# Graph layer with pre-norm on one core: layer-norm statistics, the last relu and add, and the last step of a count move from VectorE to ACT, POOL and PE

## The reference

```python
h = maximum(layernorm(x), 0)                 # eps 1e-5, over the 128 channels
mask = adj != 0
idx = the first 25 neighbours of each node, in order of their number
agg = h[idx].max(over the neighbours)        # with at most 25 neighbours also max(agg, 0)
out = x + relu(concat([h, agg], -1) @ W + b)
```

## Time and profile before

| | |
|---|---|
| median of 3 runs | 734.77 us (734.31 to 734.83) |
| profiled execution, its own time | 734.86 us |
| its span | 732.9 us |
| busy: DVE, PE, ACT, POOL | 91%, 85%, 65%, 7% of the span |
| mean granted TensorE clock | 0.971 |

### The profile page before, as it was taken

The page is one execution under the profiler, slowest core; times in us unless marked ns, Lnnn a source line. Parts: engine busy times, 40 slices in busy tenths (PEclk is TensorE's granted clock), DMA queues, the critical chain, the costliest instruction groups (busy, mean ns, idle before and its releaser), DMA issues.

```text
span 732.9 us, 10603 instructions
## 1 busy us (share of the span) xinstructions
PE 619.5 (85%) x3216; PEld 281.0 (38%) x3248; DVE 663.3 (91%) x941; ACT 476.1 (65%) x594; POOL 50.3 (7%) x41
## 2 busy tenths in 40 slices
PE   2278979899788997889899898989989898998976
PEld 2033443434334352443435343343525334353423
DVE  2559999999998999989998999989999999989996
ACT  2588568783777737775676857778478837858220
POOL 1300002000110002100030000200021000300000
PEclk9689999999999999999999999999999999999998
DMA  9240131410315103151302413141122410030100
GB/s 365 70 169 34 58 144 43 167 78 30 144 64 196 57 13 130 73 185 57 123 20 102 158 57 143 57 176 60 48 116 80 179 57 30 0 114 3 57 15 14
DMA packets 19125, 67.61 MB, mean 92 GB/s; under 512 B 4499, under 2 KB 7830, under 8 KB 16534
## 3 DMA queue, kind: packets, MB, share of 16 engines
q1 hardware_dynamic: 19094, 67.26, 24.4%
HBM read 42.08 MB, written 4.19 MB: 63 GB/s over the span
## 4 chain that ended last, share of the span: by engine, by line
DVE 40%; PE 35%; issue 17%; ACT 4%; DVEq 2%; DMA 1%; POOL 1%; ACTq 0%
DVE best L695 15%; PE picked L528 11%; PE picked L529 9%; DVE late_hot L701 7%; DVE prefix L232 5%; DVE hot L676 5%; PE ring L473 4%; PE side L487 4%; DVE best L796 4%; PE final L556 2%; PE final L560 2%; DVE late_most L681 1%; PE ring L479 1%; DVE late_other L684 1%; DMA adj_in<-in_adj_dram 1%
## 5 line engine op out<-in xcount | busy, mean ns | idle before, releaser
L695 DVE TENSOR_TENSOR best<-picked,best 128x1024 f32<-128x1024 f32 x224 | 268.8, 1217 | 22.4 <-PE picked L529 21.6
L528 PE MATMUL picked<-hot,h_hi 128*128 128x512 f16 x512 | 198.0, 387 | 57.7 <-DVE best L695 45.6
L529 PE MATMUL picked<-hot,h_lo 128*128 128x512 f16 x512 | 196.8, 384 | 0.0
L528 PE MATMUL picked<-late_hot,hi_skew 128*128 128x512 f16 x336 | 127.6, 380 | 13.0 <-DVE late_hot L701 8.6
L529 PE MATMUL picked<-late_hot,lo_skew 128*128 128x512 f16 x336 | 127.3, 379 | 0.0
L528 PEld LDWEIGHTS picked<-hot,h_hi 128*128 128x128 f16 x512 | 50.4, 98 | 160.0 <-DVE best L695 86.6
L796 DVE TENSOR_TENSOR best<-picked,best 128x1024 f32<-128x1024 f32 x84 | 102.4, 1219 | 8.4 <-PE picked L529 8.3
L361 ACT ACTIVATE rank<-ring,bias_big 128x512 bf16<-128x512 f32 x128 | 81.2, 683 | 28.5 <-PE ring L479 27.7
L400 ACT COPY best<-picked 128x1024 f32<-128x1024 f32 x32 | 32.3, 1015 | 101.9 <-PE picked L529 101.9
L676 DVE TENSOR_SCALAR hot<-rank 128x4096 f16<-128x4096 bf16 x64 | 90.1, 1409 | 7.7 <-ACT rank L361 7.7
L361 ACT ACTIVATE late_rank<-ring,late_bias 128x512 bf16<-128x512 f32 x128 | 81.0, 685 | 21.5 <-PE ring L479 15.2
(11 more groups left out here) (77 smaller groups left out, 560.6 us busy)
## 6 DMA issues: line engine op xcount, KB each, us to landing
adj_in<-in_adj_dram SPq DMA_DIRECT2D x16, 2048.0 KB, 7.9
late_skew<-late SPq DMA_DIRECT2D x32, 192.0 KB, 2.3
x_in<-in_x_dram SPq DMA_DIRECT2D x8, 512.0 KB, 8.6
xres<-in_x_dram SPq DMA_DIRECT2D x16, 256.0 KB, 7.8
late_skew<-late SPq DMA_DIRECT2D x16, 256.0 KB, 2.4
late_skew<-late SPq DMA_DIRECT2D x32, 128.0 KB, 2.0
out_dram<-xres SPq DMA_DIRECT2D x16, 256.0 KB, 2.0
late_skew<-late SPq DMA_DIRECT2D x32, 64.0 KB, 1.9
```

The lines of the kernel that those rows point to most:

```text
L528: nc.tensor.matmul(dst, hi[:, slot, k, :], onehot, start=start, stop=False)
L529: return nc.tensor.matmul(dst, lo[:, slot, k, :], onehot, start=False, stop=stop)
L695: nc.vector.tensor_tensor(best[:, half, s, :, :], picked[s][:, :, :], best[:, half, s, :, :], ALU.max).then_inc(picked_read, 1)
```

## The change

VectorE's `stats_of`, `moments_of` and `finish_group` go. ACT forms the statistics inside `spreads`: per class a Copy scaled by -1/C whose accumulator is minus the mean, then a Square with that as bias whose accumulator is the sum of squares, then the square root. It does so at the very front of its queue for batch 0, and for the next batch in the step of the even group, behind the last `make_mask` and in front of `first_maxima`. `make_gain` moves from use 8 to use 4, `relu_parts` from behind use 15 to use 8. The relu of the output is ACT's `cut_result`, last in its step, and the addition to x is POOL's `finish_group`. In the count, the four small operations into `late_other` go; PE's `tops`, behind pick 10, spreads the four partial maxima with two tiny matmuls into row 0 of `side`, and VectorE's `set_rounds` reduces these five numbers at use 11.

```diff
-    STATS_USES, MOMENTS_USE, SPREAD_USE, GAIN_USE = (4, 5), 6, 7, 8
+    GAIN_USE, RELU_USE = 4, 8
+    ROUNDS_USE = COUNT_USE + 2
...
             def normalize(batch):
                 pool.wait_ge(gain_made, 2 * batch + 2)
+                mean = minus_mean[:, :].unsqueeze(2).to_broadcast([P, K, C])
+                nc.gpsimd.tensor_tensor(h32[:, :, :], x_in[:, :, :], mean, ALU.add).then_inc(centred, 1)
...
+            def finish_group(g, s, loaded):
+                pool.wait_ge(xres_loaded[s], loaded)
+                pool.wait_ge(added_made, g + 1)
+                nc.gpsimd.tensor_tensor(xres[:, s, :], added[:, :], xres[:, s, :], ALU.add).then_inc(result_made, 1)
...
             def spreads(batch):
-                act.wait_ge(moments_made, K * batch + K)
-                nc.scalar.activation(spread[:, :], moments[:, :, 1], ACT.Sqrt, bias=bias_eps[:, 0:1]).then_inc(spread_made, 1)
+                act.wait_ge(x_loaded, 16 * batch + 16)
+                if not isinstance(batch, int) or batch > 0:
+                    act.wait_ge(lo_made, batch)
+                for k in range(K):
+                    nc.scalar.activation(h32[:, k, :], x_in[:, k, :], ACT.Copy, scale=-1.0 / C,
+                                         accum_out=minus_mean[:, k:k + 1]).then_inc(means_made, 1)
+                act.wait_ge(means_made, K * batch + K)
+                for k in range(K):
+                    nc.scalar.activation(h32[:, k, :], x_in[:, k, :], ACT.Square, bias=minus_mean[:, k:k + 1],
+                                         accum_out=squares[:, k:k + 1]).then_inc(squares_made, 1)
+                act.wait_ge(squares_made, K * batch + K)
+                nc.scalar.activation(spread[:, :], squares[:, :], ACT.Sqrt, bias=bias_eps[:, 0:1], scale=1.0 / C).then_inc(spread_made, 1)
...
+            def cut_result(g):
+                act.wait_ge(result_made, g + 1)
+                act.wait_ge(final_written, g + 1)
+                nc.scalar.activation(added[:, :], final[:, :], ACT.Relu).then_inc(added_made, 1)
...
+            spreads(0)
             for n in range(TURNS):
                 turned_mask(0, n)
...
-                    if use == SPREAD_USE and new_batch:
-                        spreads(batch)
-                if new_batch:
-                    relu_parts(batch, slot)
+                    if use == RELU_USE and new_batch:
+                        relu_parts(batch, slot)
...
+                if u % PER_BATCH == 0 and not at_end(it, u, PER_BATCH):
+                    spreads(batch_of(it, u) + 1)
                 if more:
                     for s in range(2):
                         first_maxima(g + 1, s, (u + 1) % 2)
...
+                cut_result(g)
...
+            def tops(g):
+                pe.wait_ge(late_reduced, g + 1)
+                nc.tensor.matmul(side[0:1, 0:CHAINS + 1], ones[:, 0:1], top_ones[:, :], start=True, stop=False)
+                nc.tensor.matmul(side[0:1, 0:CHAINS], late_most[:, :], eye32[:, 0:P:PART], start=False,
+                                 stop=True).then_inc(tops_written, 1)
...
                     pick_pair(g, use, slot)
                     if use == PAIRS and more:
                         lower_sums(at - TURNS)
+                    if use == COUNT_USE + 1:
+                        tops(g)
...
-            def count_rounds(g, s):
+            def count_rounds(g):
                 dve.wait_ge(count_written, g + 1)
                 nc.vector.tensor_reduce(late_most[:, :], side[:, :], AX.X, ALU.max).then_inc(late_reduced, 1)
-                dve.wait_ge(late_reduced, (CHAINS + 1) * g + 1)
-                for c in range(CHAINS):
-                    nc.vector.tensor_scalar(late_other[:, c:c + 1], late_most[c * PART:c * PART + 1, :], LINK * P / 2, 1.0, ALU.add,
-                                            ALU.max).then_inc(late_reduced, 1)
-                dve.wait_ge(late_reduced, (CHAINS + 1) * (g + 1))
-                nc.vector.tensor_reduce(late_rounds[0:1, s:s + 1], late_other[:, :], AX.X, ALU.max).then_inc(rounds_known, 1)
+
+            def set_rounds(g, s):
+                dve.wait_ge(tops_written, g + 1)
+                nc.vector.tensor_reduce(late_rounds[0:1, s:s + 1], side[0:1, 0:CHAINS + 1], AX.X, ALU.max).then_inc(rounds_known, 1)
...
-            def finish_group(g, s, loaded):
-                dve.wait_ge(final_written, g + 1)
-
-                dve.wait_ge(xres_loaded[s], loaded)
-                nc.vector.scalar_tensor_tensor(out=xres[:, s, :], in0=final[:, :], scalar=0.0, in1=xres[:, s, :],
-                                               op0=ALU.max, op1=ALU.add).then_inc(result_made, 1)
...
-            stats_of(0, range(K))
-            moments_of(0)
...
                     if use == COUNT_USE:
-                        count_rounds(g, s)
+                        count_rounds(g)
+                    if use == ROUNDS_USE:
+                        set_rounds(g, s)
...
-                    if use in STATS_USES and new_batch:
-                        half = STATS_USES.index(use)
-                        stats_of(batch, range(half * HALF, (half + 1) * HALF))
-                    if use == MOMENTS_USE and new_batch:
-                        moments_of(batch)
                     if use == GAIN_USE and new_batch:
                         make_gain(batch)
...
-                finish_group(g, s, 16 * (it * (UNROLL // 2) + u // 2 + 1))
```

More of the change, by code:

```diff
@@ L125, in build @@
         late_most = sb("late_most", [P, 1], F32)
-        late_other = sb("late_other", [1, CHAINS], F32)
+        top_ones = sb("top_ones", [P, CHAINS + 1], BF16)
         late_rounds = sb("late_rounds", [P, 2], I32)
@@ L132, in build @@
         x_in = sb("x_in", [P, K, C], F32)
-        stats = sb("stats", [P, K, 6], F32)
-        moments = sb("moments", [P, K, 2], F32)
+        minus_mean = sb("minus_mean", [P, K], F32)
+        squares = sb("squares", [P, K], F32)
         held = sb("held", [P, 4], F32)
@@ L147, in build @@
         xres = sb("xres", [P, 2, Q * C], F32)
+        added = sb("added", [P, Q * C], F32)
         picked = [psum(f"picked{s}", [P, 2, ROWS], F32) for s in range(2)]
@@ L174, in build @@
         late_reduced = sem("late_reduced")
+        tops_written = sem("tops_written")
         rounds_known = sem("rounds_known")
@@ L186, in build @@
         result_made = sem("result_made")
-        stats_made = sem("stats_made")
-        moments_made = sem("moments_made")
+        added_made = sem("added_made")
+        means_made = sem("means_made")
+        squares_made = sem("squares_made")
         spread_made = sem("spread_made")
@@ L316, in _ @@
             nc.gpsimd.affine_select(out=eye32[:, :], in_=eye32[:, :], compare_op=ALU.is_equal, base=0, **line).then_inc(basics_made, 1)
+            nc.gpsimd.memset(top_ones[:, 0:CHAINS], 1.0).then_inc(basics_made, 1)
+            nc.gpsimd.memset(top_ones[:, CHAINS:CHAINS + 1], 1.0 / P).then_inc(basics_made, 1)
             def low_part(batch, slot):
@@ L324, in normalize @@
                 pool.wait_ge(gain_made, 2 * batch + 2)
-                mean = moments[:, :, 0:1].to_broadcast([P, K, C])
-                nc.gpsimd.tensor_tensor(h32[:, :, :], x_in[:, :, :], mean, ALU.subtract).then_inc(centred, 1)
+                mean = minus_mean[:, :].unsqueeze(2).to_broadcast([P, K, C])
+                nc.gpsimd.tensor_tensor(h32[:, :, :], x_in[:, :, :], mean, ALU.add).then_inc(centred, 1)
                 pool.wait_ge(centred, batch + 1)
@@ L339, in step @@
                         low_part(batch_of(it, u + 1), ((u + 1) // PER_BATCH) % 2)
+                finish_group(g, u % 2, 16 * (it * (UNROLL // 2) + u // 2 + 1))
             over_groups(pool, step)
@@ L406, in _ @@
                 find_past(0, p)
-            spreads(0)
             relu_parts(0, 0)
@@ L583, in _ @@
             pe.wait_ge(consts_made, 10)
+            pe.wait_ge(basics_made, 15)
             def step(it, u):
@@ L654, in make_mask @@
                                         ALU.not_equal).then_inc(mask_made, 1)
[L656 to L665, removed]
             def make_gain(batch):
```

## The result

The changed kernel takes 739.66 us (738.86 to 741.62, 5 runs), the one before 734.77 (732.08 to 735.18, 5 runs): a ratio of 1.0076, 95% interval [1.0058, 1.0093], **slower by 0.76%**. The profiled execution of after has a span of 737.4 and an own time of 739.36. The forecast was 746.0. In spans, 732.9 became 737.4: +4.5, where the sum said +11.1. Executions of one kernel scatter by up to 5 us (before: near 732 and near 736, the latter with a lower granted clock), so the two are compared stretch by stretch.

The account below looks back on a forecast made before the run. PE paces up to take 5; between take 10 and the late loop VectorE and PE are nearly level. Terms 1.0 + 4.8 - 0.4 + 1.7 + 0 + 4.0 = +11.1 on 734.9 gave 746.0 us, own range 741 to 750.

Parts of the forecast that it names:

- the even groups: Count: PE stalls 0.95 at `tops`, delaying ranks and picks; +0.6 us in each of 8 even groups, +4.8.
- Rival 2: PE and ACT keep pace, VectorE alone sets the time, PE's wait at `tops` costs nothing: 727 us; chance 13%.
- The prefix sum held by POOL: Odd groups: POOL's multiplication holds the first VectorE prefix sum, adding 1.67 us, about 2.1 in all.
- Rival 1: Odd groups: POOL does not hold the prefix sum, 7 x 1.67 = 11.7 us less, 734.3 us; chance 20%.
- the odd groups behind the reduce: Late rank stages, picks and `turn_h` bring the first late take to 211.9, now 211.68: +0.24 x 7 = +1.7 us.
- the last group: The group has no ranks for `tops` to delay, so the new count gains about 0.4 us.
- the start: ACT's statistics delay `mask_t` by 7.2 us, the earlier gain returns 3.2: +4.0 (bounds +0.2 and +6.1).
- the end: ACT's relu (0.6) and POOL's add (about 1.0) with a hand-over replace VectorE's 0.69: +1.0 us.
- the accumulator's read: ACT's statistics: each accumulator read taken at 0.2 us, between 0 and 0.30, shown by no row.
- A: ACT's time for one batch's statistics: 7.8 us (4.6 to 9.4), free in even groups up to 8.5, uncovered at the start.
- Rival 3: Dear accumulator reads: beyond 8.5 us of ACT statistics, start and four even groups pay; 751 or 757 us; chance 12%.

Follow-up runs that it names:

- run 1: The changed kernel with PE's `tops` matmuls behind the rank matmuls of use 10 instead of in front: 738.16 us, ratio 1.0038 to the kernel before.
- run 6: The changed kernel with the gain at use 7, relus behind use 15 and `tops` behind the ranks of use 10: 722.92 us, ratio 0.9836.
- run 8: The kernel before with only the count's new last step, `tops` and `set_rounds`, in the change's places: 744.24 us, ratio 1.0132.
- run 2: The changed kernel with `make_gain` at use 7 and `relu_parts` back behind use 15, statistics staying on ACT: 735.66 us, ratio 0.9995.
- run 10: The changed kernel with `relu_parts` alone back behind use 15, the gain staying at use 4: 749.15 us, ratio 1.0195.
- run 3: The changed kernel with the result's relu and addition back on VectorE in one operation: 741.89 us, ratio 1.0089.
- run 7: Run 6 with the result's relu and addition and batch 0's statistics also back on VectorE: 718.61 us, ratio 0.9787.
- run 9: Run 7 with the two relus of `relu_parts` one each behind the rank stages of uses 11 and 12: 710.01 us, ratio 0.9653.
- run 4: The changed kernel with batch 0's statistics alone back on VectorE: 738.95 us, ratio 1.0057.
- Run 5: The changed kernel with eight extra unused 512-column matmuls on PE ahead of pick 8 of odd groups: 736.7 us, ratio 1.0021.

## Why the prediction came out as it did

**Direction and mechanism of the even groups: right.** PE waits 0.78 at `tops` (said: 0.95), the first late take is 0.58 later behind the reduce (said: 0.6), and runs 1, 6 and 8 show that the place of `tops` is the whole of it: behind the ranks the same count gains 0.3 in an even group (10.55 against 10.86) instead of losing 0.6. Rival 2, under which the stall costs nothing, fell.

**The prefix sum held by POOL: right.** 2.04 where 2.08 was worked out, and 0.41 again in run 2. Rival 1 fell. The rule of the Trainium skill (SBUF — State Buffer, section Who interferes with whom) that the forecast set beside the rows is borne out: the prefix sum has two SBUF inputs, POOL had issued 0.14 us earlier, and it was held until POOL was done (193.43 against 193.15).

**The step that failed is that of the odd groups behind the reduce:** "first late take at 211.9, now 211.68", +0.24 a group. It is -0.40 (step 41.65 against 42.05). Up to the reduce the forecast held: 10.83 behind the first prefix sum, measured 10.80. From the reduce on it has 12.76 (199.14 to 211.9), and 12.18 was measured. The chain of ranks, picks and `turn_h` is the one that the forecast names; two of its terms were mis-sized by 0.3 each:

```profile
204.65 2.63 ACT L374 ACTIVATE rank<-ring,bias_big 128x512 bf16<-128x512 f32 x4
...
211.57 0.60 PE L560 MATMUL side<-eye,h 128*128 128x128 f32 x4
...
212.45 0.38 PE L565 MATMUL picked<-late_hot,hi_skew 128*128 128x512 f16 x1
```

The rank stages begin 13.26 behind the first prefix sum (204.65 - 191.39), and 13.59 was forecast (201.9 - 188.31), because the forecast left the end of past 2 where it was (197.9, 9.6 behind the prefix sum) and it came 9.2 behind it. Before, ACT's late-rank stage ahead of it stood behind the square root, which waited for `moments` until 195.45; now that stage waits for PE behind pick 8 (1.16, until 198.42), and so for take 6. The forecast moved take 6 but not this stage. And `turn_h` with nothing ahead of it took 0.9 (211.57 to 212.45), not 1.2. The runs price the parts of an undisturbed odd group: -1.30 to the reduce for the statistics gone from VectorE (10.72 to 9.42, run 2), +0.6 for `tops` (run 8), +1.4 for the early gain and -1.08 for the early relus (runs 2 and 10). Their sum is so small that an error of 0.6 turns its sign: 7 x 0.64 = 4.5 us. Low clock took 0.9 of it back (-1.9 in all, not 7 x -0.40). Of the 6.6 us that the sum was too high, these groups are 3.6, the last group 1.8, the start 1.6, the even groups 0.3, and the end is -0.7.

**The last group** gained 2.2 in place of 0.4. From reduce to late it has 10.01, not 11.68, and so has run 8, with the count alone: before, PE's matmuls there ran at 1.2 GHz from 711.36 to 715.04, and with the new count they don't. How the 1.67 divides between the saved operations and the clock is shown by no run. The other 0.5 lies between the last fold of group 14 and the reduce: 14.37 in every kernel whose `finish_group` is on POOL, 14.87 in every one with it on VectorE (before, runs 3, 7, 8 and 9). In this group, where PE's queue holds no work for a next group, `finish_group` had no cover, and the forecast took it at nothing.

**The start** was mis-sized: the accumulator's read at 0.2 is 0.09 from start to start (16 x 0.11 = 1.8 of A), and x landed at 9.90, not 10.5: together +1.6 in place of +4.0. The eight `lower_sums` matmuls, at a lower clock, took 3.55 instead of 2.90, which makes it the +2.4 measured, to 0.1. That 0.65 is luck of the clock and not the change's: runs 4, 8 and 9, with VectorE's statistics at the start, have 3.62. **The end** was too cheap by 0.7: POOL's add costs 1.28, two thirds of the 1024-column one and not half, which is 0.3 of it; 0.2 is the projection, at a lower clock than before, and the rest is not divided.

**Rival 3** fell: ahead of `first_maxima` ACT still has idle time in every even group. The place of the last of the earlier trace rows, 7.97 idle then:

```profile
353.08 1.01 ACT L429 COPY best<-picked 128x1024 f32<-128x1024 f32 x1 [2.00 <-PE picked L566]
```

The 5.97 that are gone are A.

**Outside all cases** was the granted clock. Behind a wait of 3.2 us, PE's next matmuls are at 1.2 GHz in some groups and not in others, at a cost of 0.1 to 1.3 us a group in before and after, and of nearly 3 in groups 1 and 13 of run 1. Run 5 shows the cause, runs 2, 6, 7 and 9 that it goes away with the wait. Which groups are hit stays open: the wait is 3.23 in those that fall and in those that don't.

## What to carry to other kernels

A tiny matmul that waits for the vector engine is not free: it stops whatever stands behind it in PE's queue, so put it behind the work that doesn't need it. Moving these two lines was worth 12.7 us with the relus and the gain in their old places, and 1.5 with them early: an edit's price depends on what else waits in the same stretch. Where a producer is moved earlier, look which engine's SBUF operation it now lies beside, and look for holes of its own size, as run 9 does for the relus (1.56 us in each odd group). And where parts of a change show up in the wrong totals, compare the steps of the loop one by one, and the granted clock with them, before believing that an edit worked or failed.

## What the runs showed of the hardware

- The granted clock fell to the 1.2 GHz level within the loop, behind idle waits of PE of 2.4 us (before, short stretches in groups 7, 9, 11 and 13) and 3.2 us (after), and of 1.8 (run 1, groups 1 and 13); in the five kernels of runs 2, 5, 6, 7 and 9, where PE waits 1.5 to 1.7 there, it stayed at the upper level from 60 us to the end of the last late loop. At the low level 512-column matmuls are 0.43 apart, not 0.22. At the start of the kernel the first eight `lower_sums` matmuls took 2.49 or 3.6 behind ACT's statistics, and 2.9 or 3.6 behind VectorE's, with the same code up to there. Eight matmuls without a use (1.89 us), put into the wait, made the kernel 3 us faster.
- Reading ACT's accumulator is a row of 0.19 that adds 0.09 from start to start: a 128-column Copy with it comes every 0.29, a Square with a bias every 0.38.
- POOL's add of 128x512 f32 takes 1.28, its operations on 1024 columns 1.90.
- A VectorE prefix sum (two fp16/bf16 tiles in SBUF) beside POOL's 1024-column multiplication: 2.04 instead of 0.41. `late_hot` beside `low_part`: 1.59 instead of 0.74.
